# Graph attention in blocks of 1024 edges: other orders on VectorE, TensorE and ScalarE, spread factors in another PSUM bank

## The chip, the cores and the metric

The kernel runs on one core of one Trainium2 chip. The metric is the device time of one execution in microseconds (us), lower is better.

## What is computed

The reference is a two-layer graph network over 12500 nodes of 128 features and 200000 directed edges, sorted by destination. The change lies in the first layer, an attention over edges:

```
h = relu(layernorm(x))
q, k, v = h @ Wq.T, h @ Wk.T, h @ Wv.T            # 8 heads of 16
scores  = (q[dst] * k[src]).sum(-1) / 4 + edge_attr @ We.T
seg_max = segment_max(scores, dst)
ex      = exp(scores - seg_max[dst])
out     = segment_sum(v[src] * ex / segment_sum(ex, dst)[dst], dst)
x       = x + out
```

The second layer is three graph convolutions of normalised neighbour sums with batch norms. The change does not touch it.

## The kernel before

The program prepares tables (keys and values in `kv_tab`, queries in `q_tab`), then attends (`attend`, L571 to L1109), then normalises and runs the three convolutions. `attend` goes once over 196 blocks of 1024 edges, that is 8 chunks (`C`) of 128 edges. Per block SyncE loads indices, edge attributes and query rows; GpSimd (POOL) gathers the rows of `kv_tab` in 8 indirect DMAs (L744); TensorE (PE), VectorE (DVE) and ScalarE (ACT) do the rest. Sums and running maxima of a window of nodes stay in SBUF (`state` and `aux`) and are rescaled whenever a block raises a node's maximum, as in an online softmax.

The order is written out by hand. `steps(eng, total, slots, stages)` (L95) takes a list of pairs (lag, stage) per engine. In round i it emits, in the list's order, each stage for block i - lag; so every engine works in a round on up to five blocks, and each engine executes its list strictly in order. Semaphores, one per product, tie the engines together: `pe.wait_ge(sc_made, s.nth)` holds TensorE and everything behind it until VectorE has made that block's scores. `s.freed(eng, sem, depth)` waits until the buffer was read `depth` blocks ago. The loop's body holds four rounds.

The stages of a block, with the line of the instruction and the engine:

- `spread_q` L954 PE copies the queries to the edges' rows, `products` L780 DVE multiplies them by the keys (two instructions), `add_up` L787 DVE sums over 16 features, `bias` L1024 PE makes `edge_attr @ We.T`, `add_bias` L793 DVE gives the scores `sc`.
- `turn_scores` L976 PE transposes the scores, `copy_scores` L1074 ACT copies them to SBUF, `spread_scores` L999 PE (16 matrix products) spreads them against the mask of `mask` L983 PE, `run_max` L799 DVE (two halves) takes each destination's maximum `ml`.
- `own_max` L808 DVE, `spread_max` L924 PE, `above_score` L815 DVE, `exp` L1047 and L1050 ACT, `messages` L821 DVE, `sum_up` L911 PE give the block's sums per local node in bank `ps_node`.
- `near_max` L931 to L935 PE, `node_max` L828 DVE, `turn_near` L963 PE, `raise_max` L848, L849, L852 DVE bring the maximum into the running one and say by how much it rises. `scale_exp` L1056 to L1063 ACT makes the factors of the old sums. `turn_max` L968 PE, `copy_max` L1069 ACT, `give_back` L991 PE and `fall_short` L857 DVE tell how far the block's own maximum falls short, `gain_exp` L1078, L1081 ACT makes the factor of the new sums.
- `scale_nodes` L864 DVE and `copy_count` L1042 ACT scale the new sums, `spread_scale` L919 PE spreads the factors of the old ones over the features (`sf_ps`, in bank `ps_scale`), `put_nodes` L942, L943 PE puts the new sums at their nodes, `shrink` L876, L877 DVE multiplies the old sums, `merge` L884, L885 DVE adds the new ones.
- `place_one` L770 and `hot_one` L762 DVE, `turn_hot` L1010, `turn_place` L1014 PE and four ACT copies prepare the selection matrices of a block that comes in.

PSUM has eight banks; the kernel keeps two engines from touching one bank at a time by waits and by the order. `ps_scale` holds `sf_ps`, `me_ps` (L924's result) and `bias_ps`. So `spread_scale` waits for `above_made`, and `bias` waits for `scaled`, the semaphore of `shrink`. `pace` (L719) makes each of the 8 gathers wait for another event of the round, so that they are spread over it.

## Time and profile before

| | us |
|---|---|
| median of 3 runs | 6654.04 (6641.29 to 6655.65) |
| the profiled execution | 6652.28 |
| its span | 6650.5 |
| VectorE's first and last `own_max` (L808), 196 blocks | 255.4 and 3012.7 |

A row of a group reads: line, engine, operation, output<-inputs, shapes, count, then busy us, mean ns of one, and the engine's idle time just before these instructions with what ended it. "remote" is a release that the profile does not put to an instruction. A row of the timeline begins with its start in us and its duration; a row with x16 joins 16 instructions. PEld is TensorE's weight load. The ends of TensorE's instructions are modelled; a semaphore's release is recorded by itself, so that a wait can end later than the end that is shown for the matrix product it waits for.

### The profile page before, as it was taken

Reading aid. Unit: us, or ns where it says so; the run is one execution under the profiler, and the core shown is the slowest. Engines: PE = TensorE matmul, PEld = TensorE weight load, DVE = VectorE, ACT = ScalarE, POOL = GpSimd, SP = SyncE. Lnnn points to the kernel's source line nnn. Section 1 sums busy time; section 2 is a strip of 40 time slices with the busy share of each in tenths; the row PEclk is TensorE's granted clock in tenths of the full one; section 3 lists DMA queues with packets and bytes.
Section 4 is the critical chain, followed back from the end, with each engine's and each line's share of the span. In section 5 each row is a group of like instructions: output and inputs, shape, how many; then the busy total and the mean of one; then the engine's idle time right before and its main releaser. Section 6 shows DMA issues by size and latency. Waiting matters only on the chain. (4 is left out here: it accounts for less than half of the span.)

```text
span 6650.5 us, 159851 instructions
## 1 busy us (share of the span) xinstructions
PE 5406.7 (81%) x49582; PEld 3559.8 (54%) x49582; DVE 4418.8 (66%) x13500; ACT 2281.1 (34%) x5686; POOL 3152.5 (47%) x3144
## 2 busy tenths in 40 slices
PE   4587777878887788875599699998899997699995
PEld 2354444545454445554477466665466665466664
DVE  7455555555555555558799677776477776677776
ACT  3222222222222222223344233333533333433332
POOL 2455555555555555555200055553255553455552
PEclk9655555555555555555677699999999999899997
DMA  4433333333333333333333433333433333533335
GB/s 140 122 92 89 91 89 89 91 90 93 90 91 88 89 92 91 92 88 109 112 95 91 120 107 106 103 104 96 134 106 107 103 103 98 169 103 104 106 104 152
DMA packets 541998, 688.37 MB, mean 104 GB/s; under 512 B 217072, under 2 KB 427905, under 8 KB 541722
## 3 DMA queue, kind: packets, MB, share of 16 engines
q0 software_dynamic: 140208, 338.71, 18.3%
q1 hardware_dynamic: 401692, 348.45, 17.4%
q8 instruction: 49, 0.80, 0.1%
q14 instruction: 49, 0.40, 0.0%
HBM read 619.25 MB, written 67.52 MB: 103 GB/s over the span
## 5 line engine op out<-in xcount | busy, mean ns | idle before, releaser
L744 POOL DMA_INDIRECT at_kv<-kv_tab,at_idx x1568 | 1605.2, 1024 | 1169.3 <-issue 491.3
L2254 ACT ACTIVATE ag_msg<-ag_pair 128x768 bf16<-128x768 f32 x1200 | 927.9, 809 | 1582.9 <-PE ag_pair L2184 1114.8
L2193 PE MATMUL ag_sum<-ag_hot,ag_msg 128*128 128x240 bf16 x10800 | 1307.2, 268 | 91.9 <-issue 73.8
L2193 PEld LDWEIGHTS ag_sum<-ag_hot,ag_msg 128*128 128x128 bf16 x10800 | 973.5, 98 | 473.8 <-issue 395.6
L2068 POOL DMA_INDIRECT ag_spill<-g_tab,ag_idx x600 | 584.6, 974 | 1224.1 <-DMA ag_idx<-spill_tab 578.9
L2123 DVE CAST ag_msg<-ag_pair 128x768 bf16<-128x768 f32 x600 | 573.2, 955 | 582.0 <-PE ag_pair L2184 267.2
L2075 POOL DMA_INDIRECT ag_spill<-g_tab,ag_idx x750 | 726.9, 969 | 460.9 <-issue 178.1
L2184 PE MATMUL ag_pair<-xs,ag_pick 128*32 128x384 bf16 x14400 | 809.4, 331 | 135.2 <-issue 83.1
L2106 DVE TENSOR_SCALAR ag_hot<-iota_win,ag_node 128x240 bf16<-128x240 bf16 x4350 | 902.5, 290 | 1.5 <-PE ag_sum L2193 1.5
L2184 PEld LDWEIGHTS ag_pair<-xs,ag_pick 128*32 128x32 bf16 x14400 | 304.7, 95 | 447.7 <-issue 282.7
L799 DVE TENSOR_REDUCE at_ml<-at_ps_bc 128x4 f32<-128x512 f32 x392 | 252.8, 686 | 362.0 <-PE at_ps_bc L999 229.8
L999 PE MATMUL at_ps_bc<-at_sct,at_sel_head 64*128 64x128 f32 x3136 | 407.6, 438 | 11.4 <-issue 11.4
L999 PEld LDWEIGHTS at_ps_bc<-at_sct,at_sel_head 64*128 64x128 f32 x3136 | 350.0, 325 | 16.8 <-issue 12.1
L976 PE MATMUL at_ps_turn<-ident,at_sc 128*64 128x128 f32 x784 | 136.1, 440 | 242.9 <-DVE at_sc L793 227.6
L954 PE MATMUL at_ps_q<-at_qd,at_hot_b 64*128 64x512 bf16 x1176 | 283.7, 616 | 12.2 <-issue 7.1
L2096 DVE TENSOR_SCALAR ag_pick<-ag_pick,iota_p 128x1024 bf16<-128x1024 bf16 x450 | 218.4, 485 | 102.7 <-DMA ag_pick<-slot_tab 96.5
L780 DVE TENSOR_TENSOR at_prod<-at_ps_q,at_kv 128x512 f32<-128x512 f32 x392 | 252.6, 686 | 48.3 <-issue 39.4
L1056 ACT ACTIVATE at_fall<-at_drop 8x128 f32<-8x128 f32 x196 | 60.5, 308 | 641.8 <-DVE at_drop L849 559.5
L1024 PEld LDWEIGHTS at_ps_scale<-at_we,at_attr 128*128 128x128 f32 x784 | 181.1, 321 | 166.9 <-issue 99.3
L793 DVE TENSOR_TENSOR at_sc<-at_qk,at_ps_scale 128x64 f32<-128x64 f32 x196 | 42.6, 217 | 340.0 <-remote 281.2
L983 PE MATMUL at_ps_bc<-at_miss_b,at_identb 128*128 128x512 bf16 x392 | 194.9, 554 | 80.5 <-DVE at_ml L799 80.3
L2193 PE MATMUL ag_sum<-ag_hot,ag_spill 128*128 128x240 bf16 x2250 | 257.5, 267 | 0.3 <-issue 0.3
(330 smaller groups left out, 8859.7 us busy)
## 6 DMA issues: line engine op xcount, KB each, us to landing
ag_pick<-slot_tab SPq DMA_DIRECT2D x150, 768.0 KB
rk_hi_bc<-hi_tab SPq DMA_DIRECT2D x50, 896.0 KB
at_attr<-attr SPq DMA_DIRECT2D x196, 128.0 KB
at_qd<-q_tab SPq DMA_DIRECT2D x1568, 12.0 KB
at_kv<-kv_tab,at_idx POOLq DMA_INDIRECT x1568
ag_spill<-g_tab,ag_idx POOLq DMA_INDIRECT x1350
tr_dv<-dinv_tab SPq DMA_DIRECT2D x72, 256.0 KB
g_tab<-xs SPq DMA_DIRECT2D x48, 384.0 KB
```

What stands on the lines that cost most here:

```text
L744: nc.gpsimd.indirect_dma_start(kv[:, s.slot, ch, :], None, env["kv_tab"], bass.IndirectOffsetOnAxis(ap=idx[:, s.slot, ch:ch + 1], axis=0)) ...
L780: last = nc.vector.tensor_tensor(prod[:, half, :], ps_q[j][:, :].rearrange("p (c d) -> p c d", d=DIM), kv[:, k, half, 0:DIM], ALU.mult)
L799: nc.vector.tensor_reduce(ml[:, HALF * j:HALF * (j + 1)], ps_bc[j][:, :].rearrange("p (h e) -> p h e", e=P), AX.X, ALU.max).then_inc(bc_re ...
L954: last = nc.tensor.matmul(ps_q[j][:, :].rearrange("p (c d) -> p c d", d=DIM), hot_b[own, k, :], qd[own, k % 2, HALF * j:HALF * (j + 1), pa ...
L999: last = nc.tensor.matmul(ps_bc[j][:, h * P:(h + 1) * P], sel_head[own, h, :], sct[own, s.slot % 2, :], start=False, stop=h == HALF - 1, s ...
L2068: nc.gpsimd.indirect_dma_start(spill[:, k, o, :], None, table, bass.IndirectOffsetOnAxis(ap=idx[:, k, o:o + 1], axis=0)).then_inc(tail_in[ ...
L2075: nc.gpsimd.indirect_dma_start(spill[:, k, o, :], None, table, bass.IndirectOffsetOnAxis(ap=idx[:, k, o:o + 1], axis=0)).then_inc(spill_in ...
L2106: last = nc.vector.tensor_scalar(hot[:, k, ch, :], env["iota_win"][:, :], node[:, k, ch:ch + 1], None, ALU.is_equal)
L2123: nc.vector.tensor_copy(msg[:, p % 4, :, :], pair_ps[p % 3][:, :, 0:3 * DIM]).then_inc(copied[p], 1)
L2184: last = nc.tensor.matmul(pair_ps[p % 3][at, ch % 2, 0:3 * DIM], pick[:, k, ch * P + j * CAP:ch * P + (j + 1) * CAP], xs[:, (P // CAP) * c ...
L2193: last = nc.tensor.matmul(sum_ps[k][:, 0:WIN], row[:, part * DIM:(part + 1) * DIM], hot[:, k, ch, :], start=first and part == 0, stop=end ...
L2254: nc.scalar.activation(msg[:, p % 4, :, :], pair_ps[p % 3][:, :, 0:3 * DIM], ACT.Copy).then_inc(copied[p], 1)
```

## The change

The stage lists of VectorE, TensorE and ScalarE are put in another order, and what this needs is added:

- `bias` stands right behind `near_max` instead of behind `spread_q`, and no longer waits for `scaled`; `add_bias` stands right behind `add_up`.
- `sf_ps` moves from bank `ps_scale` to `ps_node`, beside the sums, `num_ps` and `den_ps` move within it. `spread_scale` waits for `nodes_made` and `count_copied` instead of `above_made`, and `shrink` waits for `placed` (L943) instead of `scale_spread` (L919).
- `turn_scores` stands ahead of `spread_q` and `turn_max`; `spread_scores` ahead of `give_back`.
- `fall_short` goes from lag 3 to lag 4 and stands behind the next round's `run_max`; so does `gain_exp`. `ml` has two buffers.
- `copy_scores` stands ahead of `scale_exp`. Two of `pace`'s events are others.

```diff
@@ -611,7 +611,7 @@
         qk = tile("qk", [P, C * HEADS])
         sc = tile("sc", [P, SLOTS, C * HEADS])
         sct = tile("sct", [P, 2, P])
-        ml = tile("ml", [P, HEADS])
+        ml = tile("ml", [P, 2, HEADS])
         md = tile("md", [P, C, HEADS])
         above = tile("above", [P, C * HEADS])
         below = tile("below", [P, C * HEADS])
@@ -633,10 +633,10 @@
         ps_node, ps_scale, ps_turn, ps_max = (psum("ps_" + s) for s in ("node", "scale", "turn", "max"))
         node_ps, near_ps = ps_node[:, 0:MSG], ps_max[:, 0:64].rearrange("p (h c) -> p h c", h=HEADS)
         mt_ps, back_ps, mbt_ps = ps_max[:, 64:72], ps_max[:, 72:80], ps_max[0:HEADS, 128:256]
-        sf_ps = ps_scale[:, 0:128]
+        sf_ps = ps_node[:, 144:272]
         me_ps, bias_ps = ps_scale[:, 384:448], ps_scale[:, 448:512]
         hot_ps, place_ps, sct_ps = ps_turn[:, 0:128], ps_turn[:, 128:256], ps_turn[:, 256:384]
-        num_ps, den_ps = ps_node[:, 256:384], ps_node[AUXD:AUXROWS, 384:512]
+        num_ps, den_ps = ps_node[:, 272:400], ps_node[AUXD:AUXROWS, 0:128]
 
         made, we_in, tables, moved = (sem(s) for s in ("made", "we_in", "tables", "moved"))
         idx_in = [sem(f"idx_in{k}") for k in range(SLOTS)]
@@ -725,13 +725,13 @@
                     if ch == 2:
                         s.freed(pool, prod_made, 2)
                     if ch == 3:
-                        s.freed(pool, near_read, 3)
+                        s.freed(pool, nodes_made, 4)
                     if ch == 4:
                         s.freed(pool, qk_made, 2)
                     if ch == 5:
                         s.freed(pool, m_kept, 3)
-                    if ch == 6 and not (isinstance(s.n, int) and s.n < 4):
-                        pool.wait_ge(added, 2 * (s.nth - 4))
+                    if ch == 6:
+                        pool.wait_ge(hot_made, s.nth)
                     if ch == 7:
                         s.freed(pool, msg_made, 3)
 
@@ -795,8 +795,8 @@
                 def run_max(j):
                     def run(s):
                         dve.wait_ge(bc_made[j], s.nth)
-                        s.freed(dve, short_made, 1)
-                        nc.vector.tensor_reduce(ml[:, HALF * j:HALF * (j + 1)],
+                        s.freed(dve, short_made, 2)
+                        nc.vector.tensor_reduce(ml[:, s.slot % 2, HALF * j:HALF * (j + 1)],
                                                 ps_bc[j][:, :].rearrange("p (h e) -> p h e", e=P), AX.X, ALU.max
                                                 ).then_inc(bc_read[j], 1)
                     return run
@@ -805,7 +805,7 @@
                     for j in range(2):
                         dve.wait_ge(bc_read[j], s.nth)
                     s.freed(dve, near_made, 1)
-                    nc.vector.tensor_tensor(md[:, :, :], ml[:, :].unsqueeze(1).to_broadcast([P, C, HEADS]),
+                    nc.vector.tensor_tensor(md[:, :, :], ml[:, s.slot % 2, :].unsqueeze(1).to_broadcast([P, C, HEADS]),
                                             env["mask_c"][:, :].unsqueeze(2).to_broadcast([P, C, HEADS]), ALU.mult
                                             ).then_inc(md_made, 1)
 
@@ -854,7 +854,7 @@
                 def fall_short(s):
                     dve.wait_ge(m_back, s.nth)
                     s.freed(dve, less_made, 1)
-                    nc.vector.tensor_tensor(short[:, :], back_ps, ml[:, :], ALU.subtract).then_inc(short_made, 1)
+                    nc.vector.tensor_tensor(short[:, :], back_ps, ml[:, s.slot % 2, :], ALU.subtract).then_inc(short_made, 1)
 
                 def scale_nodes(s):
                     k = s.slot % 2
@@ -867,7 +867,7 @@
                                             ).then_inc(nodes_made, 1)
 
                 def shrink(s):
-                    dve.wait_ge(scale_spread, s.nth)
+                    dve.wait_ge(placed, s.nth)
                     dve.wait_ge(den_scale_made, s.nth)
                     if not (isinstance(s.n, int) and s.n < 1):
                         dve.wait_ge(added, 2 * (s.nth - 1))
@@ -885,10 +885,9 @@
                     nc.vector.tensor_tensor(den, den, den_ps, ALU.add).then_inc(added, 1)
 
                 steps(dve, sh.BLOCKS, SLOTS, [
-                    (3, run_max(0)), (3, run_max(1)), (3, own_max), (2, products), (3, above_score),
-                    (4, scale_nodes), (4, load_bases), (3, node_max), (2, add_up), (3, load_first), (4, shrink),
-                    (3, raise_max), (2, add_bias), (4, merge), (0, place_one), (0, hot_one),
-                    (3, messages), (3, fall_short)], w)
+                    (3, run_max(0)), (3, run_max(1)), (4, fall_short), (3, own_max), (2, products), (3, above_score),
+                    (3, node_max), (4, scale_nodes), (4, load_bases), (2, add_up), (2, add_bias), (4, shrink),
+                    (3, load_first), (3, raise_max), (4, merge), (0, place_one), (0, hot_one), (3, messages)], w)
                 dve.wait_ge(added, 2 * (w + 1) * sh.BLOCKS)
                 next_pass(nc, dve, sh, env, (turn, wrap, by, step), (moved, tables), w)
 
@@ -915,7 +914,8 @@
 
                 def spread_scale(s):
                     pe.wait_ge(scale_made, s.nth)
-                    pe.wait_ge(above_made, s.nth if isinstance(s.n, int) and s.n == sh.BLOCKS - 1 else s.nth + 1)
+                    pe.wait_ge(nodes_made, s.nth)
+                    pe.wait_ge(count_copied, s.nth)
                     nc.tensor.matmul(sf_ps, sel_feat[:, :, :].rearrange("h d e -> h (d e)"), scale[:, :], start=True,
                                      stop=True).then_inc(scale_spread, 1)
 
@@ -1018,17 +1018,15 @@
                     k = s.slot
                     pe.wait_ge(attr_in[k], 16 * s.use)
                     s.freed(pe, above_made, 1)
-                    if not (isinstance(s.n, int) and s.n < 2):
-                        pe.wait_ge(scaled, 2 * (s.nth - 2))
                     for j in range(J):
                         last = nc.tensor.matmul(bias_ps[:, j * 32:(j + 1) * 32], att[:, k, j, :], we[:, :],
                                                 start=True, stop=True)
                     last.then_inc(bias_made, 1)
 
                 steps(pe, sh.BLOCKS, SLOTS, [
-                    (2, mask(0)), (2, mask(1)), (3, spread_max), (3, near_max), (4, spread_scale), (4, put_nodes),
-                    (3, turn_near), (1, spread_q), (2, bias), (3, turn_max), (2, turn_scores), (3, give_back),
-                    (2, spread_scores), (0, turn_hot), (0, turn_place), (3, sum_up)], w)
+                    (2, mask(0)), (2, mask(1)), (3, spread_max), (3, near_max), (2, bias), (3, turn_near),
+                    (4, spread_scale), (4, put_nodes), (2, turn_scores), (1, spread_q), (3, turn_max),
+                    (2, spread_scores), (3, give_back), (0, turn_hot), (0, turn_place), (3, sum_up)], w)
 
         @block.scalar
         def _(act):
@@ -1106,8 +1104,8 @@
                     nc.scalar.activation(place_t[:, s.slot, :], place_ps, ACT.Copy).then_inc(place_copied, 1)
 
                 steps(act, sh.BLOCKS, SLOTS, [
-                    (3, exp), (4, copy_count), (3, scale_exp), (3, copy_max), (2, copy_scores), (0, cast_place),
-                    (3, gain_exp), (0, copy_hot), (0, copy_place), (0, widen_hot)], w)
+                    (4, gain_exp), (3, exp), (4, copy_count), (2, copy_scores), (3, scale_exp), (3, copy_max),
+                    (0, cast_place), (0, copy_hot), (0, copy_place), (0, widen_hot)], w)
 
 
 def normalise(nc, sh, env):
```

VectorE's queue in the loop, the difference from `above_score` (lag 3) to `shrink` (lag 4); rows with ISA are the sequencer's:

```order
 L815 TENSOR_TENSOR at_above<-at_sc,at_ps_scale 128x64
+L828 TENSOR_REDUCE at_top_n<-at_ps_max 128x8
 L864 TENSOR_TENSOR at_nodes<-at_ps_node,at_gain 128x136
 L532 TENSOR_LOAD first_i
-L828 TENSOR_REDUCE at_top_n<-at_ps_max 128x8
 L787 TENSOR_REDUCE at_qk<-at_prod 128x64
+L793 TENSOR_TENSOR at_sc<-at_qk,at_ps_scale 128x64
 L876 ISA
-L876 TENSOR_TENSOR state<-state,at_ps_scale 128x128
+L876 TENSOR_TENSOR state<-state,at_ps_node 128x128
 L877 ISA
 L877 TENSOR_TENSOR aux<-aux,at_scale_d 9x128
```

L793 leaves its place behind `raise_max` for one ahead of `shrink`.

TensorE's queue in the loop, the difference from `near_max` (lag 3) to `spread_q` (lag 1). Line numbers behind the removed wait fall by two (L1024 is L1022, L911 is L910):

```order
 L935 MATMUL at_ps_max<-at_md,at_place 128x64
-L919 MATMUL at_ps_scale<-at_scale,at_sel_feat 128x128
+L1022 MATMUL at_ps_scale<-at_we,at_attr 128x32 x2
+L963 MATMUL at_ps_max<-ident,at_top_n 8x128
+L919 MATMUL at_ps_node<-at_scale,at_sel_feat 128x128
 L942 MATMUL at_ps_node<-at_place,at_nodes 128x128
 L943 MATMUL at_ps_node<-at_place,at_nodes 9x128
-L963 MATMUL at_ps_max<-ident,at_top_n 8x128
+L976 MATMUL at_ps_turn<-ident,at_sc 64x128 x2
 L948 REGISTER_ALU
 L949 ISA
 L954 MATMUL at_ps_q<-at_qd,at_hot_b 128x512 x6
```

The bias product stands seven rows earlier, `turn_near` ahead of the three products of the old and new sums, and the scores' transposition (L976) directly behind them.

What follows on the same queue:

```order
-L1024 MATMUL at_ps_scale<-at_we,at_attr 128x32 x2
 L966 REGISTER_ALU
 L968 MATMUL at_ps_max<-ident,at_mnew 128x8
-L976 MATMUL at_ps_turn<-ident,at_sc 64x128 x2
+L999 MATMUL at_ps_bc<-at_sct,at_sel_head 128x128 x8
 L991 MATMUL at_ps_max<-at_m_node,at_place_t 128x8
-L999 MATMUL at_ps_bc<-at_sct,at_sel_head 128x128 x8
```

Between the queries' products (L954) and the spreading of the scores (L999) only `turn_max` (L968) is left.

## Rows read from the trace of the kernel before

**Rows 1.** The instructions of L808, one per block, whole trace: min/median/max ns, first and last start.

```profile
L808 DVE TENSOR_TENSOR at_md<-at_ml,mask_c x196: 224/226/268, 255.4 to 3012.7; 128x64 f32<-128x64 f32 x196
```

**Rows 2.** Groups on VectorE from 1000 to 3000 us.

```profile
L799 DVE TENSOR_REDUCE at_ml<-at_ps_bc 128x4 f32<-128x512 f32 x282 | 181.9, 686 | 248.2 <-PE at_ps_bc L999 161.5 <-issue 60.3 <-remote 25.7
...
L848 DVE TENSOR_TENSOR at_mnew<-aux,at_ps_max 8x128 f32<-8x128 f32 x141 | 38.8, 275 | 108.4 <-remote 61.8 <-PE at_ps_max L963 25.3 <-issue 19.4
...
L828 DVE TENSOR_REDUCE at_top_n<-at_ps_max 128x8 f32<-128x64 f32 x141 | 31.3, 222 | 81.2 <-remote 66.4 <-PE at_ps_max L935 9.5 <-issue 5.3
L793 DVE TENSOR_TENSOR at_sc<-at_qk,at_ps_scale 128x64 f32<-128x64 f32 x142 | 30.9, 217 | 245.9 <-remote 203.0 <-PE at_ps_scale L1024 28.9 <-issue 14.1
...
L857 DVE TENSOR_TENSOR at_short<-at_ps_max,at_ml 128x8 f32<-128x8 f32 x142 | 23.6, 167 | 12.8 <-remote 7.4 <-PE at_ps_max L991 1.2
```

**Rows 3.** Busy time by stretch: PE, PEld, DVE, ACT, POOL, granted clock, DMA share, GB/s.

```profile
1000.00:3000.00 2000.00, 1607.44 (x9331) 997.11 (x9329) 1171.08 (x2967) 565.61 (x2263) 1151.81 (x1125) 0.56 0.33 90
1502.00:1505.00 3.00, 3.00 (x24) 2.45 (x22) 1.84 (x5) 0.98 (x4) 2.17 (x2) 0.50 0.25 66
1506.00:1509.00 3.00, 2.13 (x12) 1.39 (x12) 2.83 (x8) 0.87 (x5) 2.18 (x3) 1.00 0.49 118
```

**Rows 4.** Timeline of one quick block, 1504 to 1518 us.

```profile
1504.75 1.29 DVE L799 TENSOR_REDUCE at_ml<-at_ps_bc 128x4 f32<-128x512 f32 x2 [1.13 <-issue]
...
1506.95 0.46 PE L935 MATMUL at_ps_max<-at_md,at_place 128*128 128x64 f32 x2
...
1508.00 0.45 PE L919 MATMUL at_ps_scale<-at_scale,at_sel_feat 8*128 8x128 f32 x2 [0.60 <-issue]
1508.11 1.21 DVE L787 TENSOR_REDUCE at_qk<-at_prod 128x64 f32<-128x1024 f32 x1
...
1509.12 0.59 PE L943 MATMUL at_ps_node<-at_place,at_nodes 128*9 128x128 f32 x2
...
1509.64 0.38 PE L963 MATMUL at_ps_max<-ident,at_top_n 128*8 128x128 f32 x1
...
1512.15 0.28 DVE L848 TENSOR_TENSOR at_mnew<-aux,at_ps_max 8x128 f32<-8x128 f32 x1 [2.32 <-remote]
...
1513.64 0.22 DVE L793 TENSOR_TENSOR at_sc<-at_qk,at_ps_scale 128x64 f32<-128x64 f32 x1 [0.62 <-PE at_ps_scale L1024]
...
1514.10 0.69 PE L976 MATMUL at_ps_turn<-ident,at_sc 128*64 128x128 f32 x4 [1.09 <-DVE at_sc L793]
...
1515.25 2.08 PE L999 MATMUL at_ps_bc<-at_sct,at_sel_head 64*128 64x128 f32 x16
...
1517.36 1.29 DVE L799 TENSOR_REDUCE at_ml<-at_ps_bc 128x4 f32<-128x512 f32 x2 [1.13 <-issue]
```

**Rows 5.** Timeline of a later block, 1538 to 1543 us.

```profile
1539.34 1.06 PE L1024 MATMUL at_ps_scale<-at_we,at_attr 128*128 128x32 f32 x4
...
1540.33 0.27 PE L968 MATMUL at_ps_max<-ident,at_mnew 8*128 8x8 f32 x1
...
1542.63 0.22 DVE L793 TENSOR_TENSOR at_sc<-at_qk,at_ps_scale 128x64 f32<-128x64 f32 x1 [3.53 <-remote]
```

**Rows 6.** The same timeline, TensorE only, 1543 to 1555 us.

```profile
1543.09 0.69 PE L976 MATMUL at_ps_turn<-ident,at_sc 128*64 128x128 f32 x4 [2.49 <-DVE at_sc L793]
...
1546.26 0.29 PE L1010 MATMUL at_ps_turn<-at_ident,at_hot 128*128 128x128 bf16 x1
...
1547.67 0.13 PEld L983 LDWEIGHTS at_ps_bc<-at_miss_b,at_identb 128*128 128x128 bf16 x2 [0.42 <-issue]
...
1550.32 0.76 PE L919 MATMUL at_ps_scale<-at_scale,at_sel_feat 8*128 8x128 f32 x2 [0.48 <-DVE at_above L815]
...
1554.96 0.27 PE L968 MATMUL at_ps_max<-ident,at_mnew 8*128 8x8 f32 x1
```

**Rows 7.** The gathers on GpSimd from 1000 to 3000 us.

```profile
L744 POOL DMA_INDIRECT at_kv<-kv_tab,at_idx x1125 | 1151.8, 1024 | 838.3 <-issue 352.0 <-DVE aux L885 267.9 <-DVE at_ml L799 142.1
```

**Rows 8.** Timeline of the block after the quick one, 1522 to 1527 us.

```profile
1522.52 0.42 PE L943 MATMUL at_ps_node<-at_place,at_nodes 128*9 128x128 f32 x2
...
1526.38 0.28 DVE L848 TENSOR_TENSOR at_mnew<-aux,at_ps_max 8x128 f32<-8x128 f32 x1 [2.33 <-remote]
```

## The prediction

> **What bounds the kernel now.** First, where the time of the changed stage lies. The source view of L808, which runs once per block, shows 196 starts from 255.4 to 3012.7 us [rows 1]: 2757.3 us over 195 intervals, 14.14 us per block. Nothing outside this loop changes, so each 1 us per block is worth 196 us.
>
> Next, who is busy in it. From 1000 to 3000 us, some 141.5 blocks, TensorE is busy 80%, VectorE 1171.1 us or 8.3 us per block, GpSimd 1151.8 us [rows 3]. No engine is full, so the round is a loop of waits between engines. The groups on VectorE say which: its idle time lies before L799 (248.2 us in 141 rounds, 1.76 us each), L793 (245.9 in 142, 1.73 us), L848 (108.4, 0.77 us) and L828 (81.2, 0.58 us) [rows 2]. All four wait for TensorE: for the spread scores, the bias product, the turned maximum and the near maximum.
>
> Last, the timeline. In a quick block the round, from one L799 to the next, takes 12.61 us [rows 4]. The scores' path is: L787 ends at 1509.32, L793 comes only at 1513.64, then L976, the ScalarE copy and L999 from 1515.25, and L799 at 1517.36. So L793 stands 4.3 us behind the sums it adds to, behind shrink, raise and the bias product. In a slower block the bias product's four products end at 1540.40 by the model of the trace, yet L793 starts at 1542.63, 2.2 us later, released by a semaphore that is recorded late [rows 5]. Such **late releases** come from TensorE alone in what I read: L963 ends at 1510.02 and L848 starts at 1512.15 [rows 4]; L943 ends at 1522.94 and L848, which waits for the product behind it, starts at 1526.38 [rows 8]. I don't know their cause. Mean round 14.14, quick round 12.61: they cost some 1.5 us per block, and they are the main doubt below.
>
> **The change part by part.** Instructions are neither added nor removed: the same 16 products of L999, the same eight gathers. Everything is order.
>
> *Bias forward, add_bias forward.* Without the wait for the previous shrinks, the bias product can start behind L935, which ends at 1507.41, 2.66 us after L799's start; its 1.06 us [rows 4, 5] end at 3.7. VectorE is done with L787 at 4.57 [rows 4], plus 0.17 for L857, which now stands in between [rows 2]. So L793 comes at some 4.8 us instead of 8.9 (1513.64 less 1504.75). The 1.73 us of waiting before it shrink to at most 0.2: **-1.5 us**. Its cover is a slack of 1 us, less than the late release of [rows 5], hence the 0.2.
>
> *turn_near forward, spread factors and put_nodes behind it.* L963 is released earlier, so L848's 0.77 us go. But shrink (L876) now waits for L943 where it waited for L919. In the quick block L943 ends at 1509.71, 4.96 us after L799; L828 ahead of L864 adds 0.22 [rows 2, 4]; at the lower clock L919 alone takes 0.76 instead of 0.45 us [rows 4, 6]. That is 5.5, against 5.0 for the end of L793: 0.5 us of plain waiting, plus L943's own lateness, which I take at the 0.77 us that L848 shows now. 1.3 less 0.77: **+0.5 us**. Queued behind this wait are the raise (L848), with it L968 and, behind L968, L999. Before, L943 was awaited only by merge (L884), behind L793, where its lateness was covered.
>
> *turn_scores ahead of spread_q.* L976 can start at about 5.5 instead of 9.35 us (1514.10). What it now does not wait for is the bias; what stands between it and L999 are the six products of L954 and L968. ScalarE's copy of the scores is covered by them. L799's wait of 1.76 us keeps its late part and loses little of the plain part, which is 1.13 us in the quick block [rows 4]: between 0 and 0.7, I take **-0.1**, since L999 still stands behind L968 and that behind the raise.
>
> *fall_short, gain_exp one round later.* 0.17 us of L857 and the two ScalarE steps move to where VectorE reads L799's result anyway; L864, which needs the gain, comes over 2 us later. 0. Two buffers of `ml` cost nothing. *Pacing*: two of eight gathers wait for other events of the same round; 0. GpSimd's floor is (1151.8 + 352.0) / 1125 x 8 = 10.7 us per block, taking the idle time that no wait explains as its own [rows 7].
>
> Sum: -1.5 + 0.5 - 0.1 = -1.1 us per block, x196 = -216 us. Against the profiled execution's 6652.3 us (span 6650.5; 1.7 us under the median of the runs) that is 6436.
>
> **How far it can go at most.** TensorE's own work bounds the new round. From L976 to the next L976, at the lower clock: 1543.09 to 1546.26, then 1546.26 to the start of L968 at 1554.96, then 0.25 us for L968, together 12.1; less the gaps before L983's loads (0.42) and L919 (0.48) it is 11.2 us [rows 6]. GpSimd's 10.7 is under it. 14.14 - 11.2 = 2.9 us per block, -576 us, 6076: the low end if no release came late. The high end of this sum is the same with L943 fully late (3.4 us in [rows 8]), priced below.
>
> A row on the clock: in the attention stretch TensorE is granted 0.56 on average, 0.50 at 1502 to 1505 though it is busy all 3 us there, and 1.00 at 1506 to 1509, behind that dense piece [rows 3]; these are its 1.2 and 2.4 GHz. The new order closes gaps, so more of the stretch may run at 2.4 GHz. The Trainium skill (TensorE: Matmul & The Clock Gate, section "Part 1: The HAM clock gate") says the throttled state is the default and that activity releases it. By that rule, and the trace agrees in that the full clock follows a dense piece, an order that keeps TensorE busier gains twice.
>
> **The rivals.**
>
> *A: the floor is reached, or the clock rises.* TensorE's late releases vanish with the new order, or the products run at 2.4 GHz for longer. For it: two of the four waits were for products issued into a full queue. Against: 80% busy already grants only 0.56. Without late releases 11.2 us per block, 6076; with a rising clock GpSimd's 10.7 holds it, 5978. With a third of the lateness left some 6180. Chance 0.13.
>
> *B: the lateness only moves.* TensorE gets denser, and if releases lag because it is dense, each wait that goes returns before L876 or L799. Then 14.1 us stay, 6640 to 6665. For it: only the last in a row of late products is waited for, and the old order hid L943's. Against: L793's is the largest single one. Chance 0.08.
>
> *C: slower, through shrink's wait for L943.* The late release of L943 now stands ahead of shrink, raise, L968 and L999 in every block, and L976's, behind L943 on the same queue, is late with it. Price: 11.2 + 3.4 [rows 8] + the late part of L799's wait (1.76 - 1.13 = 0.63) = 15.2 us per block, 1.1 more than now: 6652 + 216 = 6868. It decides from a lateness of 14.14 - 11.2 - 0.63 = 2.3 us per block on. For it: [rows 8]. Against: L848, behind the same stretch, waits only 0.77 us on average. Chance 0.13.
>
> That the order does not come out as written can be left aside: it is static.
>
> **How the numbers follow.** Forecast 0.66, by itself 6300 to 6560 (1.8 to 0.5 us per block); A 0.13, B 0.08, C 0.13. About 0.2%, or 13 us, is what a measurement of this kernel can tell from no change. Faster: 0.66 + 0.13 + 0.02 of B = 0.81; same 0.05; slower 0.01 of B + 0.13 = 0.14. The time is the likeliest case's, 6436. The range takes in A's upper part and B: 6170 to 6655; out of it are C and the rest of A, together some 0.19.
>
> **What would show it.** Right: L808's starts span some 2545 us; the idle time before L793 falls under 0.3 us per block; before L876 a new wait of about 1.3 us for TensorE stands and L848's is gone; L799's wait is 1.5 to 1.8 us. A: L876's wait under 0.6, granted clock over 0.65 for the clock half. B: L799 and L876 together wait over 4 us. C: L876 waits over 2.5 us. Wrong altogether: a long wait of GpSimd or of VectorE for gathers (L780), or ScalarE's copy of the scores late because `exp` stands ahead of it.

## The result: 2.3% slower, and the profile after

The changed kernel takes 6812.36 us in the median (6804.13 to 6818.62, 4 runs), the kernel before on the same chip 6654.84 (6641.29 to 6667.66, 4 runs). The ratio is 1.0227, 95% interval 1.0212 to 1.0242. The forecast was 6436 us, in a range of 6170 to 6655. The profiled execution takes 6818.62 us, its span is 6816.9 us.

The loop alone explains it. This is the source view of L808 in the changed kernel, the answer to [rows 1]:

```profile
L808 DVE TENSOR_TENSOR at_md<-at_ml,mask_c x196: 224/226/227, 255.6 to 3174.0; 128x64 f32<-128x64 f32 x196
```

That is 2918.4 us over 195 intervals, 14.97 us per block where it was 14.14, so 161 of the 166 us between the two profiled spans (6816.9 and 6650.5), some 0.83 us per block.

The groups on VectorE from 1000 to 3000 us, 133 rounds, the answer to [rows 2]:

```profile
L799 DVE TENSOR_REDUCE at_ml<-at_ps_bc 128x4 f32<-128x512 f32 x266 | 177.9, 689 | 94.3 <-PE at_ps_bc L999 58.7 <-remote 28.6 <-issue 5.4
L787 DVE TENSOR_REDUCE at_qk<-at_prod 128x64 f32<-128x1024 f32 x133 | 162.2, 1220 | 49.9 <-issue 49.9
L876 DVE TENSOR_TENSOR state<-state,at_ps_node 128x128 f32 x134 | 38.7, 289 | 205.5 <-PE at_ps_node L943 180.3 <-remote 24.2 <-issue 1.0
L848 DVE TENSOR_TENSOR at_mnew<-aux,at_ps_max 8x128 f32<-8x128 f32 x134 | 36.9, 275 | 4.2
L793 DVE TENSOR_TENSOR at_sc<-at_qk,at_ps_scale 128x64 f32<-128x64 f32 x133 | 29.3, 221 | 4.5
L815 DVE TENSOR_TENSOR at_above<-at_sc,at_ps_scale 128x64 f32<-128x64 f32 x133 | 29.3, 220 | 431.6 <-remote 431.6
L828 DVE TENSOR_REDUCE at_top_n<-at_ps_max 128x8 f32<-128x64 f32 x133 | 29.0, 218 | 4.5 <-remote 4.0 <-PE at_ps_max L935 0.2
```

The two groups of the kernel before that the rows ahead of the prediction do not show:

```profile
L876 DVE TENSOR_TENSOR state<-state,at_ps_scale 128x128 f32 x141 | 39.4, 279 | 11.8 <-remote 7.3 <-issue 3.6 <-PE at_ps_scale L919 0.7
L815 DVE TENSOR_TENSOR at_above<-at_sc,at_ps_scale 128x64 f32<-128x64 f32 x141 | 30.4, 216 | 52.4 <-PE at_ps_scale L924 33.9 <-remote 18.6
```

Divided by the rounds, the idle time of VectorE in front of each line is:

| us per round | before | after |
|---|---|---|
| L793, bias product | 1.73 | 0.03 |
| L799, spread scores | 1.76 | 0.71 |
| L848, turned maximum | 0.77 | 0.03 |
| L828, near maximum | 0.58 | 0.03 |
| L787, unexplained ("issue") | 0.00 | 0.38 |
| L876, old and new sums at their nodes | 0.08 | 1.53 |
| L815, each edge's maximum (`spread_max`, L924) | 0.37 | 3.25 |

The first four lose 4.0 us and the last three gain 4.7: net 0.7 of the 0.83 us (L857's wait adds 0.1, from 12.8 to 28.3 us in all). What the 0.38 us before L787 are, no row says. Four waits that the change aimed at are gone or halved, L876 has the wait that was predicted, and **one wait that the prediction has no term for, L815's, eats all of it**. TensorE stands still for the same reason, in front of the bias product (group on TensorE, same stretch):

```profile
L1022 PE MATMUL at_ps_scale<-at_we,at_attr 128*128 128x32 f32 x532 | 136.0, 396 | 505.5 <-DVE at_above L815 503.9 <-issue 1.2
```

3.8 us per round. The stretch as a whole, the answer to the first row of [rows 3]: TensorE is busy 1393.75 us where it was busy 1607.44, 70% instead of 80%, yet its mean granted clock is higher, 0.65 instead of 0.56. The higher clock came without a gain, and not from a TensorE that is busier on average.

```profile
1000.00:3000.00 2000.00, 1393.75 (x8790) 851.88 (x8788) 1125.30 (x2799) 518.98 (x2131) 1018.83 (x1065) 0.65 0.31 85
```

GpSimd is no bound: its gathers wait 980.2 of the 2000 us, 617.4 of it for two of VectorE's results, as in [rows 7].

```profile
L744 POOL DMA_INDIRECT at_kv<-kv_tab,at_idx x1065 | 1019.2, 957 | 980.2 <-DVE at_nodes L864 334.2 <-issue 314.7 <-DVE aux L852 283.2
```

One round in the timeline of the changed kernel, 1515 to 1525 us, where [rows 4, 5] show the old order:

```profile
1515.22 0.28 ACT L1072 ACTIVATE at_sct<-at_ps_turn 128x128 f32<-128x128 f32 x1 [8.20 <-remote]
1515.56 2.08 PE L999 MATMUL at_ps_bc<-at_sct,at_sel_head 64*128 64x128 f32 x16 [3.05 <-ACT at_sct L1072]
...
1519.06 1.16 PE L910 MATMUL at_ps_node<-at_msg,at_hot_w 128*32 128x137 f32 x16
1520.16 1.04 PE L983 MATMUL at_ps_bc<-at_miss_b,at_identb 128*128 128x512 bf16 x2
1520.99 0.53 PE L924 MATMUL at_ps_scale<-at_md,at_hot_t 128*128 128x64 f32 x2
...
1524.08 0.22 DVE L815 TENSOR_TENSOR at_above<-at_sc,at_ps_scale 128x64 f32<-128x64 f32 x1 [2.79 <-remote]
```

L924 ends at 1521.52 by the model; VectorE, which has nothing else to do, is released at 1524.08, 2.56 us later. Only then can L1022 start, since it writes the bank that L815 reads. So the bias product, the transposition of the near maximum and all behind them begin when the lateness has run out.

L924 is only where the lateness is waited for. The recorded changes of the semaphores put it further up the queue: L924's change comes 0.06 us (median of 127 rounds from 1000 to 3000 us) behind that of the block's sums (L910), though the two mask products and L924 itself lie between them and the modelled ends are 1.52 us apart. Between the change of L1014, ahead of L910's 16 products, and L910's own lie 3.07 us where the modelled ends have 1.02 (79 rounds; the trace lacks some of these changes).

### The profile page after: what moved, and what is told of

Same layout as the page of the kernel before. It is cut to its first block and busy times, and to the rows that moved or that the text cites. A ratio compares the mean times of both kernels' runs of the same rounds, so it can differ in the third digit from the quotient of the medians.

```text
span 6816.9 us, 159528 instructions
## 1 busy us (share of the span) xinstructions
PE 5227.8 (77%) x49582; PEld 3431.9 (50%) x49582; DVE 4446.7 (65%) x13500; ACT 2261.2 (33%) x5686; POOL 3047.7 (45%) x3144
## 5 line engine op out<-in xcount | busy, mean ns | idle before, releaser
L744 POOL DMA_INDIRECT at_kv<-kv_tab,at_idx x1568 | 1501.3, 957 | 1438.3 <-DVE at_nodes L864 482.7
L1022 PE MATMUL at_ps_scale<-at_we,at_attr 128*128 128x32 f32 x784 | 200.1, 395 | 734.4 <-DVE at_above L815 732.5
L1022 PEld LDWEIGHTS at_ps_scale<-at_we,at_attr 128*128 128x128 f32 x784 | 179.9, 319 | 764.9 <-issue 764.6
L815 DVE TENSOR_TENSOR at_above<-at_sc,at_ps_scale 128x64 f32<-128x64 f32 x196 | 43.2, 220 | 626.6 <-remote 625.8
L999 PE MATMUL at_ps_bc<-at_sct,at_sel_head 64*128 64x128 f32 x3136 | 363.1, 400 | 7.9 <-ACT at_sct L1072 6.2
L799 DVE TENSOR_REDUCE at_ml<-at_ps_bc 128x4 f32<-128x512 f32 x392 | 261.9, 689 | 159.9 <-PE at_ps_bc L999 84.6
L1086 ACT ACTIVATE at_hot_b<-at_ps_turn 128x128 bf16<-128x128 f32 x196 | 54.4, 278 | 866.8 <-remote 709.3
L999 PEld LDWEIGHTS at_ps_bc<-at_sct,at_sel_head 64*128 64x128 f32 x3136 | 314.8, 295 | 12.6 <-ACT at_sct L1072 6.6
L954 PE MATMUL at_ps_q<-at_qd,at_hot_b 64*128 64x512 bf16 x1176 | 285.9, 621 | 4.6 <-DMA at_qd<-q_tab 4.6
L787 DVE TENSOR_REDUCE at_qk<-at_prod 128x64 f32<-128x1024 f32 x196 | 239.1, 1220 | 72.5 <-issue 72.5
L1072 ACT ACTIVATE at_sct<-at_ps_turn 128x128 f32<-128x128 f32 x196 | 54.4, 278 | 691.7 <-PE at_ps_turn L976 468.6
L780 DVE TENSOR_TENSOR at_prod<-at_ps_q,at_kv 128x512 f32<-128x512 f32 x392 | 252.5, 686 | 47.9 <-issue 39.7
```

Source lines behind the costliest of these rows:

```text
L744: nc.gpsimd.indirect_dma_start(kv[:, s.slot, ch, :], None, env["kv_tab"], bass.IndirectOffsetOnAxis(ap=idx[:, s.slot, ch:ch + 1], axis=0)) ...
L799: nc.vector.tensor_reduce(ml[:, s.slot % 2, HALF * j:HALF * (j + 1)], ps_bc[j][:, :].rearrange("p (h e) -> p h e", e=P), AX.X, ALU.max).th ...
L954: last = nc.tensor.matmul(ps_q[j][:, :].rearrange("p (c d) -> p c d", d=DIM), hot_b[own, k, :], qd[own, k % 2, HALF * j:HALF * (j + 1), pa ...
L999: last = nc.tensor.matmul(ps_bc[j][:, h * P:(h + 1) * P], sel_head[own, h, :], sct[own, s.slot % 2, :], start=False, stop=h == HALF - 1, s ...
L1022: last = nc.tensor.matmul(bias_ps[:, j * 32:(j + 1) * 32], att[:, k, j, :], we[:, :], start=True, stop=True)
```

## Experiments

The first suspicion was that the lateness is a matter of how densely TensorE is fed in the new order. Each run below was measured against the kernel before on its own chip, and that turned out to be needed. In the cuts of the code, "..." stands for lines left out, and the stage lists are shortened.

**1. Four versions of the changed kernel on one chip.** e1: give_back ahead of the spreading of the scores again:

```diff
-                    (2, spread_scores), (3, give_back), (0, turn_hot), (0, turn_place), (3, sum_up)], w)
+                    (3, give_back), (2, spread_scores), (0, turn_hot), (0, turn_place), (3, sum_up)], w)
```

> The changed kernel with give_back (L991) ahead of spread_scores (L999) on TensorE again, as it was before the change. Theory D (dense): TensorE's releases come late when TensorE runs a long stretch without a gap up to L910, and the granted clock goes to full in the same stretch. Here L999 waits for ScalarE's L1067 ahead of it, a gap of about 1 us that the changed kernel does not have. D expects the release of L924, and so the idle time before L815 (431.6 us in 133 rounds, 3.2 us each), to fall below 2 us per block and the time to be 6650 to 6790. Rival P (position): the wait of bias (L1022) for above_made, in the middle of the round, is what costs; it is untouched here, so the gap adds to the round: 6812 plus up to 1.0 x 196, that is 6850 to 7010.

e2: the bias product, the scores' transposition and add_bias in their old places, the rest as changed (TensorE's list; on VectorE add_bias goes back behind raise_max):

```diff
-                    (3, near_max), (2, bias), (3, turn_near),
-                    (4, spread_scale), (4, put_nodes), (2, turn_scores), (1, spread_q), (3, turn_max),
+                    (3, near_max), (3, turn_near),
+                    (4, spread_scale), (4, put_nodes), (1, spread_q), (2, bias), (3, turn_max), (2, turn_scores),
```

> The changed kernel with bias behind spread_q, turn_scores behind turn_max, and add_bias behind raise_max, as before the change; the bank of the spread factors, fall_short's lag, the ScalarE order and give_back behind L999 stay as changed. Theory D (late releases come from the uninterrupted stretch of TensorE from L1022 to L910, which is broken again by the wait of L976 for add_bias): idle time before L815 under 1 us per block, time 6600 to 6720. Rival P (the bias product's wait for above_made costs by itself): the same direction, 6600 to 6720. Rival F (the fault lies in the parts kept here: shrink waiting for L943, give_back or fall_short): 6780 or more.

e3: a gap ahead of the spreading of the scores, which waits for the merge of the same round:

```diff
                     pe.wait_ge(sct_made, s.nth)
+                    if not (isinstance(s.n, int) and s.n < 2):
+                        pe.wait_ge(added, 2 * (s.nth - 2))
```

> The changed kernel, where spread_scores (L999) waits in addition for the merge of the same round (L885). This only adds a wait, about 0.8 us of TensorE gap ahead of L999. Theory D: the gap shortens the dense stretch, releases of L910 and L924 come less late, so the idle time before L815 falls by more than 1 us per block and the kernel is not slower, 6650 to 6815, although a wait was added. Rival P or any theory in which a wait only adds: 6812 + 0.8 x 196 = 6970 (6900 to 7000), L815's idle time unchanged or lower only by what the round grows.

e4: six more mask products between near_max and the bias product (they write once more what the masks wrote):

```diff
-                    (3, near_max), (2, bias), (3, turn_near),
+                    (3, near_max), (2, refill), (2, bias), (3, turn_near),
```

> The changed kernel with six more matrix products per block (the mask's two products repeated three times, same result) ahead of the bias product, where TensorE stands idle 3.8 us per block. At 1.2 GHz they take 6 x 0.43 = 2.6 us. Theory D: the stretch gets still denser; the granted clock of the attention rises over 0.75 from 0.65. If late releases come with the change of clock, they shrink once the clock stays full: 6500 to 6800; if they come with density itself they grow: over 6900. Rival P (the engine is simply idle there): the six products fit into the idle time and the time stays within 1% of 6812.

Measured: the kernel before takes 5763.27 us on this chip, 13% under the 6654.84 of the first. Ratios to it: e1 1.0059 (1.0030 to 1.0089), e2 1.0504 (1.0475 to 1.0534), **e3 0.9767** (0.9738 to 0.9796), e4 0.9892 (0.9863 to 0.9921). The source views of L808 give 11.11, 12.44, 10.30 and 10.68 us per block, all well under 14. L815, which waited 3.25 us per round on the first chip, does not wait at all (group of e1 from 800 to 2100 us):

```profile
L815 DVE TENSOR_TENSOR at_above<-at_sc,at_ps_scale 128x64 f32<-128x64 f32 x116 | 24.3, 209 | 0.0
```

e4 adds work to TensorE and runs at a granted clock of 0.93 (800 to 2100 us); VectorE's longest wait is then the one for the gathers, 1.3 us per round:

```profile
L780 DVE TENSOR_TENSOR at_prod<-at_ps_q,at_kv 128x512 f32<-128x512 f32 x244 | 168.0, 691 | 163.7 <-DMA at_kv<-kv_tab,at_idx 142.1 <-issue 19.2
```

What follows: nothing yet about the loss on the first chip, since the chip was another and the changed kernel itself was not among the four. But the condition came into sight.

**2. The two kernels themselves, on another chip,** and the gap once more.

> The kernel before once more, unchanged, for its trace. In the last call the kernel before took 5763 us where it had taken 6654, and the four traces of that call show no late release of TensorE at all. Theory L (late releases are a state of the chip, not of the kernel): this run takes either 5730 to 5790 with releases within 0.1 us of the modelled ends and 11.0 us per block, or 6640 to 6670 with late ones and 14.1 us per block, nothing between. Rival M (the late releases come and go within a run, or another cause made the time shorter): something between, or 5763 with late releases.

> The changed kernel, unchanged, beside the kernel before on one chip. Theory L: without late releases the new order works as the layout said: the idle time before L793 is under 0.2 us per block, the round is 10.3 to 10.9 us against 11.0, ratio 0.975 to 0.997. With late releases the ratio is 1.02 as measured first. Theory D, in which the stretch up to L910 costs by itself: ratio over 1.01 on either.

> The changed kernel with spread_scores waiting for the merge, once more, to compare it with the changed kernel on one chip (they never ran side by side). Theory W (a wait only adds): 0.3 to 0.8 us per block more than the changed kernel, 60 to 160 us. Theory G (the gap helps by itself, by keeping L999 and what follows off something): faster than the changed kernel by over 20 us.

Measured: the kernel before against itself 5754.94 us, 0.9997 (0.9978 to 1.0015); **the changed kernel 5640.74 us, 0.9801** (0.9782 to 0.9819); with the gap 5623.13 us, 0.9777 (0.9761 to 0.9793). The same two programs, 2.3% slower on the first chip, 2.0% faster here. The kernel before from 800 to 2100 us, 118 rounds:

```profile
L799 DVE TENSOR_REDUCE at_ml<-at_ps_bc 128x4 f32<-128x512 f32 x238 | 153.4, 686 | 97.2 <-PE at_ps_bc L999 93.7
L876 DVE TENSOR_TENSOR state<-state,at_ps_scale 128x128 f32 x118 | 32.8, 278 | 0.0
L848 DVE TENSOR_TENSOR at_mnew<-aux,at_ps_max 8x128 f32<-8x128 f32 x118 | 32.5, 276 | 39.2 <-PE at_ps_max L963 36.9
L793 DVE TENSOR_TENSOR at_sc<-at_qk,at_ps_scale 128x64 f32<-128x64 f32 x118 | 26.1, 221 | 121.1 <-PE at_ps_scale L1024 119.9
L815 DVE TENSOR_TENSOR at_above<-at_sc,at_ps_scale 128x64 f32<-128x64 f32 x119 | 25.0, 210 | 0.0
```

The changed one, same stretch, 124 rounds:

```profile
L780 DVE TENSOR_TENSOR at_prod<-at_ps_q,at_kv 128x512 f32<-128x512 f32 x248 | 167.9, 690 | 72.4 <-DMA at_kv<-kv_tab,at_idx 50.2 <-issue 19.3
L799 DVE TENSOR_REDUCE at_ml<-at_ps_bc 128x4 f32<-128x512 f32 x248 | 159.8, 686 | 29.5 <-PE at_ps_bc L999 27.2 <-issue 0.2
L876 DVE TENSOR_TENSOR state<-state,at_ps_node 128x128 f32 x124 | 35.8, 289 | 121.7 <-PE at_ps_node L943 120.2 <-issue 1.1
L793 DVE TENSOR_TENSOR at_sc<-at_qk,at_ps_scale 128x64 f32<-128x64 f32 x123 | 27.2, 221 | 4.2
L815 DVE TENSOR_TENSOR at_above<-at_sc,at_ps_scale 128x64 f32<-128x64 f32 x124 | 26.1, 211 | 0.0
```

Per round: L793 1.03 to 0.03, L799 0.82 to 0.24, L848 0.33 to 0.03, against L876 0.0 to 0.98 and some 0.4 more before L780. That sums to -0.5, and the round went from 11.00 to 10.51 us. No release of TensorE is "remote" in these rows: what the profile calls the end of a product is when it is released. Theory L holds in this: whether releases come late goes with the chip, or with its state at that time, and not with the kernel. Each chip was met once, so the runs do not tell a lasting property of the chip from a passing one. I call such chips prompt and the others late. The gap (r_gap) met neither expectation: it neither added 60 us nor took off 20, but took off 18.

**3. What a denser TensorE costs, and parts of the change.** Six more mask products directly ahead of spread_max, in the kernel before and in the changed one:

```diff
-                    (2, mask(0)), (2, mask(1)), (3, spread_max),
+                    (2, mask(0)), (2, mask(1)), (2, refill), (3, spread_max),
```

> The kernel before with the mask's two products repeated three times ahead of spread_max (L924): six more products of 512 columns per block, 2.6 us at 1.2 GHz and 1.3 at 2.4, the same result. They put off the releases of L924, L935 and all behind them by that much, in every block: a stand-in, on any chip, for what the late releases did at this place. Theory S (the old order has slack behind L924, the new one none): 0.6 to 1.6 us per block more than the kernel before, ratio 1.02 to 1.055. Rival E (both orders bear a delay there alike): 1.3 to 2.6 us per block, ratio 1.045 to 1.09.

> The changed kernel with the same six products at the same place. Theory S: the delay goes through L815, L828, L787, L793 and L876 to the raise and L999 in full, 1.3 to 2.6 us per block, so that the lead of 2% over the kernel before turns into a lag behind the slowed kernel before: its ratio lies above that of s_before_slow. Rival E: it lies 0.02 below that of s_before_slow, as the unslowed kernels do.

e5: the kernel before with the bank of the spread factors (and num_ps, den_ps in theirs) and the waits moved as in the change, no order touched. The bias product's wait for `scaled` goes too, so "the bank alone" below stands for bank and waits:

```diff
-        sf_ps = ps_scale[:, 0:128]
+        sf_ps = ps_node[:, 144:272]
...
-                    dve.wait_ge(scale_spread, s.nth)
+                    dve.wait_ge(placed, s.nth)
...
-                    pe.wait_ge(above_made, s.nth if isinstance(s.n, int) and s.n == sh.BLOCKS - 1 else s.nth + 1)
+                    pe.wait_ge(nodes_made, s.nth)
+                    pe.wait_ge(count_copied, s.nth)
...
-                    if not (isinstance(s.n, int) and s.n < 2):
-                        pe.wait_ge(scaled, 2 * (s.nth - 2))
```

> The kernel before with the bank of the spread factors changed alone: sf_ps beside the sums, spread_scale waits for nodes_made and count_copied, shrink waits for placed, bias without its wait for scaled; all orders as before. By the prediction's account this part alone costs: shrink, with the raise behind it, now waits for L943. 0.2 to 1.3 us per block more than before, ratio 1.01 to 1.045. Rival: the part is free, since turn_near follows put_nodes in this order anyway and the raise waits for it: within 0.3%.

The gap (e3) again:

> The changed kernel with spread_scores waiting for the merge, for the chip of this call. If the kernel before takes 5730 to 5790 here: 5615 to 5635, as on two other chips. If it takes over 6600 (late releases): theory D (a gap ahead of L999 keeps the clock from rising in the dense stretch and with it the late releases away) says below 6812 by over 50; theory W (a wait only adds) says 6812 or more.

Measured, on a late chip (kernel before 6579.68 us; one of its 13 executions took 9554.91, unexplained, which the median does not feel): the filled kernel before 1.0003 (0.9992 to 1.0013), the filled changed one 1.0175 (1.0141 to 1.0208), **the bank alone 0.9923** (0.9898 to 0.9948), the gap 1.0252 (1.0231 to 1.0273). The gap, which on a prompt chip is 0.3% under the changed kernel, does nothing against the loss here: its 6739.02 us lie under the 6812 of its expectation only because the kernel before is 1.1% quicker on this chip than on the first. Theories S and E both fail in size, for the filled kernel before lost nothing where 2% to 9% were expected; S is right in the order of the two, the filled changed kernel being the slower by 1.7%, but so is the changed kernel without the filling (2.3% on the first chip). The bank alone is a miss too: expected to cost 1.0% to 4.5%, it gains 0.8%. The filled kernel before is granted a clock of 0.78 from 1000 to 3000 us, more than the changed kernel's 0.65, and loses nothing. So the granted clock by itself is not the condition. Its L815 waits 1.53 us per round, but L793's wait has shrunk to 0.23:

```profile
L815 DVE TENSOR_TENSOR at_above<-at_sc,at_ps_scale 128x64 f32<-128x64 f32 x143 | 31.6, 221 | 219.5 <-PE at_ps_scale L924 90.1 <-issue 86.4 <-remote 42.8
L793 DVE TENSOR_TENSOR at_sc<-at_qk,at_ps_scale 128x64 f32<-128x64 f32 x142 | 29.1, 205 | 33.3 <-PE at_ps_scale L1031 17.6 <-remote 13.5 <-issue 2.2
```

In the kernel with the bank alone L876 waits 1.41 us per round for the placed sums (L944 there), which is what the prediction gave the change, while L793 keeps 118.6 of 245.9 us and L848 10.1 of 108.4 (against the kernel before on the first chip).

```profile
L876 DVE TENSOR_TENSOR state<-state,at_ps_node 128x128 f32 x142 | 40.8, 287 | 199.8 <-PE at_ps_node L944 178.9 <-remote 17.9 <-issue 3.0
```

**4. Which part loses.** f1: the changed kernel again, for the scale of the others:

> The changed kernel once more, as the measure for the three beside it. On a chip where TensorE's releases come late (kernel before near 6600 us): 1.02, with some 3 us before L815 per round. On a chip where they come on time (kernel before near 5760 us): 0.98, and nothing before L815.

f2: bank and bias alone, that is e5 and in it:

```diff
-                    (3, near_max), (4, spread_scale),
+                    (3, near_max), (2, bias), (4, spread_scale),
...
-                    (1, spread_q), (2, bias), (3, turn_max),
+                    (1, spread_q), (3, turn_max),
...
-                    (3, node_max), (2, add_up), (3, load_first), (4, shrink),
-                    (3, raise_max), (2, add_bias), (4, merge)
+                    (3, node_max), (2, add_up), (2, add_bias), (3, load_first), (4, shrink),
+                    (3, raise_max), (4, merge)
```

> The kernel before with the spread factors' bank and waits moved, the bias product directly behind near_max and add_bias behind add_up, all else in the old order. Theory T1 (the loss on a late chip is the bias product's wait for above_score, which holds TensorE's queue while L924's release is late): late chip 1.01 to 1.03, L815 over 2.5 us per round; prompt chip 0.97 to 0.99. Theory T2 (the loss lies in the other orders: turn_near forward, the scores' turn ahead of spread_q, fall_short later): late chip 0.98 to 0.995, L815 under 1.5 us; prompt chip about 1.00.

f3: the rest without the bias part and without turn_scores forward (the kernel of e2, on this chip):

> The changed kernel with bias, turn_scores and add_bias back in their old places, as once before on a prompt chip, where it took 1.050. T1: on a late chip the change without its bias part stands under the change itself, at 0.99 to 1.01. T2: it is as slow as the change or slower, 1.02 to 1.06, since bank and the other orders stay. Prompt chip: 1.05 again.

f4: the changed kernel with the bias product at the head of the round:

```diff
-                    (2, mask(0)), (2, mask(1)), (3, spread_max), (3, near_max), (2, bias), (3, turn_near),
+                    (2, bias), (2, mask(0)), (2, mask(1)), (3, spread_max), (3, near_max), (3, turn_near),
...
-                    s.freed(pe, above_made, 1)
+                    s.freed(pe, above_made, 2)
```

> The changed kernel with the bias product ahead of the mask products, at the head of the round, waiting only for the above_score of the round before. T1: TensorE's queue no longer stands behind L815: late chip 0.97 to 0.995, TensorE's idle time before the bias product under 0.3 us per round; prompt chip 0.975 to 0.985, as the change. T2: late chip 1.02, L815 still near 3 us; prompt chip 0.98 to 0.99.

The chip was a late one (kernel before 6583.36 us):

| kernel | ratio to before (95%) | L815, L876, L799: wait, us per round |
|---|---|---|
| f1, as changed | 1.0235 (1.0218 to 1.0253) | 3.21, 1.47, 0.67 |
| **f2, bank and bias alone** | **0.9864** (0.9847 to 0.9882) | 0.14, 1.92, 2.26 |
| f3, all but bias and turn_scores | 1.0117 (1.0099 to 1.0134) | 1.00, 1.09, 1.65 |
| f4, bias at the head | 1.0078 (1.0059 to 1.0097) | 2.58, 0.98, 1.26 |

Three rows carry the verdict. Of f2, 1000 to 3000 us:

```profile
L815 DVE TENSOR_TENSOR at_above<-at_sc,at_ps_scale 128x64 f32<-128x64 f32 x141 | 29.7, 211 | 19.3 <-remote 14.8 <-PE at_ps_scale L925 4.6
```

Of f4, VectorE:

```profile
L815 DVE TENSOR_TENSOR at_above<-at_sc,at_ps_scale 128x64 f32<-128x64 f32 x140 | 30.6, 218 | 361.5 <-remote 361.4
```

Of f4, TensorE:

```profile
L963 PE MATMUL at_ps_max<-ident,at_top_n 128*8 128x128 f32 x141 | 51.5, 366 | 415.2 <-DVE at_top_n L828 404.5 <-issue 10.6
```

T1, that the bias product's wait for L815 is what loses, does not hold by itself: f2 has this wait and gains 1.4%, L815 waits 0.14 us. T2, that the other orders lose, stands: f2 is within its numbers, f3 is slower than before, though by 1.2% and not by the 2% that T2 named. From f2 to f1, which adds only the other orders, it is 1.0235/0.9864 = 1.038, some 240 us or 1.2 us per block. f4 meets neither theory's time and shows both at once: out of L815's way the bias product takes the ratio from 1.0235 to 1.0078, so that given the late L924 two thirds of the loss hang on its place. TensorE's wait before it is 7.6 us in all. But the wait for the late L924 is still 2.6 us, and it now holds TensorE at L963, whose input VectorE makes behind L815.

**5. Which of the other orders.** g1: the changed kernel with turn_scores back; g2: the kernel of f2 with turn_scores forward; and g3, a candidate: e5 with the bias product at the head as in f4 and add_bias behind add_up. First g1:

```diff
-                    (4, spread_scale), (4, put_nodes), (2, turn_scores), (1, spread_q), (3, turn_max),
-                    (2, spread_scores),
+                    (4, spread_scale), (4, put_nodes), (1, spread_q), (3, turn_max), (2, turn_scores),
+                    (2, spread_scores),
```

> The changed kernel with turn_scores alone back behind spread_q and turn_max; the bias product stays forward. Theory T3 (the loss on a late chip comes from turn_scores ahead of spread_q: the queries' products, the spread scores, the block's sums, the masks and L924 then run as one dense piece, the granted clock rises and L924's release comes late): late chip 0.98 to 1.00, L815 under 1.5 us per round, granted clock under 0.60. Theory T4 (the loss comes from turn_near ahead of the three products and the shift of VectorE's order around them): late chip 1.01 to 1.03 still, clock near 0.60. Prompt chip: 0.99 to 1.01.

Then g2, against f2:

```diff
-                    (3, turn_near), (1, spread_q), (3, turn_max), (2, turn_scores), (3, give_back),
+                    (3, turn_near), (2, turn_scores), (1, spread_q), (3, turn_max), (3, give_back),
...
-                    (3, scale_exp), (3, copy_max), (2, copy_scores),
+                    (2, copy_scores), (3, scale_exp), (3, copy_max),
```

> The kernel before with the bank, the bias product and add_bias moved (0.986 on a late chip), plus turn_scores ahead of spread_q and copy_scores ahead of scale_exp. T3: late chip 1.00 to 1.03, L815 over 2 us per round, clock 0.61 or more. T4: 0.97 to 0.99, L815 under 0.5 us, clock under 0.60. Prompt chip: 0.97 to 0.98.

> The kernel before with the bank moved and the bias product at the head of the round, in TensorE's wait for the maxima to be read, where it costs no wait for above_score; add_bias behind add_up. The candidate that should beat both: late chip 0.97 to 0.985 (f2's 0.986 less the bias product's 1 us between near_max and spread_scale, part of which VectorE's wait for L944 shows), prompt chip 0.96 to 0.98. Rival: the products at the head push L925 and L944 back as much as they free, then 0.985 to 1.00.

They ran on a prompt chip (before 5764.23 us): g1 1.0011 (0.9993 to 1.0029), g2 0.9956 (0.9939 to 0.9973), g3 1.0058 (1.0037 to 1.0079). On such chips the change is worth nothing without turn_scores forward (g1, 1.0011) and nothing without spread_scores ahead of give_back (e1, 1.0059), and 0.9801 with both (three chips, each against its own kernel before). g2's 0.9956, slower than expected, says that turn_scores forward brings little without turn_near forward and the rest. g3 is a miss as a candidate, by its rival's bounds too. **Which of the other orders brings the lateness in front of L815 on a late chip stays open**; T3 and T4 were not told apart, since no run of g1 or g2 fell on a late chip. What points to turn_scores are f2, f3 and f4 on one late chip: without it forward L815 waits 0.14 and 1.00 us per round, with it 2.58 and, in f1, 3.21. But f3's 1.00 us come without it, and no run there moves it alone.

## Why the prediction was wrong

*The waits on the bias.* "The 1.73 us of waiting before it shrink to at most 0.2: -1.5 us." The wait shrank to 0.03, on every chip. Its worth did not follow. On a late chip the step from e5 to f2 is 0.9923 to 0.9864 (two chips, each against its own kernel before), 0.6% or 39 us, 0.2 us per block: L793's wait goes from 118.6 us to 10.9, but L876's rises from 199.8 to 274.5 and L799's from 220.3 to 319.3.

*Shrink's wait for L943.* "+0.5 us", made of a wait of 1.3 less L848's 0.77. Right in both parts, 1.53 and 0.74. On a late chip the bank and its waits alone are a gain of 0.8%, with L793's wait halved, in part because the bias product no longer waits for `scaled`; there the part is a gain, where its own term made it a cost.

*turn_near and turn_scores forward.* "Between 0 and 0.7, I take -0.1", and L848's wait goes. **This is the step that failed.** Bounded at zero from above, it measured +1.2 us per block on a late chip (f2 to f1), together with fall_short, gain_exp, give_back and copy_scores, which the prediction had at nothing. Its plain parts came true: L848 and L828 wait for nothing, and L799 lost 1.05 us and waits 0.71, where the prediction had it stay at 1.5 to 1.8. What has no term is L815. The prediction read its 0.37 us nowhere and looked for the next late wait only at L876 and L799. But on VectorE the work between L808 and L815 is only L780's two halves; when the lateness in front of L924 grew beyond their 1.4 us, all of it was waiting, and VectorE's L828, L864, L787 and L793 and TensorE's L1022 stood behind it.

*The lateness as a stock.* The sum took 1.5 us of lateness per block as given, and let single portions of it vanish with the wait in which they showed. The recorded changes of L924's semaphore against its modelled end say otherwise (some changes are missing from each late trace): the median is 0.9 us in the kernel before, 4.4 in the changed one, 0.0 in f2, 1.3 in f3, 3.8 in f4, and 0.0 in both kernels on a prompt chip. It depends on the order. L943's, on which rival C rested, has a median of only 0.4 us in the kernel before, since the 3.4 of [rows 8] was a single block, and of 0.0 in the changed one.

*Rival C* had the sign, the kind of mechanism and nearly the size (15.2 us per block, measured 14.97), but not the place: its own test, L876 over 2.5 us, shows 1.53. "It decides from a lateness of 2.3 us on" was met by L815's 3.25. *Rival B* (L799 and L876 together over 4 us; measured 2.24) fell as well, though its thought, that each wait that goes returns, is what f2 shows. *Rival A*'s clock did rise to 0.65, its threshold, without any gain; what the prediction made of the Trainium skill (TensorE: Matmul & The Clock Gate, section "Part 1: The HAM clock gate"), that an order that keeps TensorE busier gains twice, was not put to the test, since this order left TensorE less busy, 70% for 80%.

*The floor.* "11.2 us per block" was undercut on prompt chips: the changed kernel takes 10.51 there, and the kernel before 11.00. It was read from a piece at the lower clock, of a late chip; with the granted clock at 0.74 (changed kernel, 800 to 2100 us) more of the products run at the higher one and are shorter.

*The condition.* Without late releases the terms have the forecast signs, but not the sizes: -1.0 for L793 (-1.5), -0.3 for L848 (-0.77), -0.6 for L799 (-0.1), +1.0 for L876 (+1.3), and +0.4 for the gathers (L780), which the prediction had priced at nothing. They add up to -0.5 where -1.1 was forecast, and 0.9801 was measured there where 0.967 was forecast. That 0.9801 lies nearer to the forecast than 1.0227 is in part luck: L799's term came out six times as large as it was put. The doubt was named as the main one; its weight, 0.13 for C, was too small, since a resource whose rule was unknown stood in all four waits that the sum was made from.

## What to carry to other kernels

When waits end later than the profile's ends of the products, the cause moves with the order: price the lateness in front of every consumer that has little work ahead of it, not only where it shows now. What may help, and was not tried here, is to put other work (here L787, 1.2 us) between the instruction that feeds a late product and the one that reads it. And before a change of some per cent is kept or thrown away, run it against the old kernel on more than one chip: here the sign depended on it. On the one late chip where it ran f2 beats both kernels (0.9864 of the kernel before, 0.964 of the changed one); on prompt ones the changed kernel with the gap does (0.9777, and 5623.13 against 5640.74 us); no version was found that does so on both, and f2 was not tried on a prompt chip.
